# KAN window layer: identity sum of the K1 part as runs, the K2 part added by VectorE, SiLU in place on the columns-first copy, and another instruction order

## The reference

```
def _fastkan(x, ln_g, ln_b, ws, wb, bb):
    ln = _layernorm(x, ln_g, ln_b)
    basis = jnp.exp(-((ln[..., None] - GRID) / DENOM) ** 2)      # 8 bases
    return basis.reshape(*basis.shape[:-2], -1) @ ws.T + jax.nn.silu(x) @ wb.T + bb
...
y = _layernorm(wins, pn_g, pn_b)                                # windows of 8 x 8 pixels, PN
a = fastkan K1 of y, regrouped along the rows of a window
d = fastkan K2 of y, regrouped along the columns of a window
e = fastkan K3 of y
z = fastkan K4 of (a + d + e)
out = z + wins
```

## Time and profile before

| | us |
|---|---|
| median of 3 runs | 11005.96 |
| lowest and highest | 11001.5, 11026.69 |
| the profiled execution's own time | 10993.59 |
| its span, first to last instruction | 10991.8 |

### The profile page before, as it was taken

One profiled execution on the slowest core, in us unless ns is written; L12 is line 12 of the kernel. 1 busy time (PEld: TensorE's weight loads), 2 busy tenths in 40 slices (PEclk: granted clock), 3 DMA queues, 4 the chain that ended last, 5 costly groups with the idle time before them and its releaser, 6 DMA issues. The chain is left out here.

```text
span 10991.8 us, 350519 instructions
## 1 busy us (share of the span) xinstructions
PE 9088.7 (83%) x158376; PEld 4584.7 (42%) x158376; DVE 8630.6 (79%) x7794; ACT 7545.8 (69%) x5712; POOL 0.2 (0%) x4
## 2 busy tenths in 40 slices
PE   0898879996665798788888888888888888888788
PEld 0344333333443686344444444444444444444344
DVE  6777756666776587688888888888888888888788
ACT  0555545554552554688888888878888888887689
POOL 0000000000000000000000000000000000000000
PEclk9999989997887999799999999999999999999899
DMA  7999879995673586455555555555555555555566
GB/s 287 250 259 257 234 217 264 266 259 214 271 276 107 171 278 227 93 105 110 112 112 106 107 105 106 105 108 109 109 111 106 105 106 109 109 110 94 159 208 203
DMA packets 1196529, 1825.48 MB, mean 166 GB/s; under 512 B 135328, under 2 KB 956448, under 8 KB 1124768
## 3 DMA queue, kind: packets, MB, share of 16 engines
q1 hardware_dynamic: 1195040, 1803.05, 64.6%
HBM read 717.78 MB, written 411.04 MB: 103 GB/s over the span
## 5 line engine op out<-in xcount | busy, mean ns | idle before, releaser
L2008 DVE SCALAR_TENSOR_TENSOR ex<-ratio,ex 128x2048 f32<-128x2048 f32 x1536 | 3504.4, 2290 | 226.7 <-ACT ratio L1910 134.7
L2129 PE MATMUL out<-ex,kan_basis 32*32 32x512 f32 x65536 | 2563.7, 624 | 321.8 <-DVE ex L2008 129.2
L2129 PEld LDWEIGHTS out<-ex,kan_basis 32*32 32x32 f32 x65536 | 1073.3, 105 | 1466.3 <-issue 801.5
L556 PE MATMUL conv<-uc,w 128*32 128x512 f32 x12288 | 1447.4, 597 | 17.1 <-DMA uc<-u 16.6
L1902 ACT ACTIVATE ex<-ex 128x2048 f32<-128x2048 f32 x512 | 975.6, 1905 | 2.9
L463 ACT ACTIVATE v<-conv,cb 128x512 f32<-128x512 f32 x512 | 350.8, 685 | 905.9 <-PE conv L556 414.5
L556 PEld LDWEIGHTS conv<-uc,w 128*32 128x32 f32 x12288 | 483.1, 109 | 735.4 <-issue 678.0
L2262 DVE TENSOR_TENSOR d<-xt 128x2313 f32<-128x2313 f32 (+2 forms) x256 | 621.7, 2494 | 83.3 <-PE acc L2316 82.9
L2316 PE MATMUL acc<-d,weights 32*32 32x512 f32 x16384 | 627.5, 600 | 70.9 <-issue 64.2
L1896 ACT ACTIVATE ex<-kin,offset 128x2048 f32<-128x2048 f32 x256 | 511.3, 1997 | 130.5 <-PE out L2129 115.0
L2080 PE MATMUL norm<-sq,c_kan_ones 128*32 128x128 f32 x10240 | 393.5, 297 | 212.1 <-DVE z L1984 151.3
(11 more groups left out here) (276 smaller groups left out, 14899.0 us busy)
## 6 DMA issues: line engine op xcount, KB each, us to landing
uc<-u SPq DMA_DIRECT2D x2048, 129.0 KB, 3.6
xt<-in_x SPq DMA_DIRECT2D x128, 1024.0 KB, 7.4
t<-v SPq DMA_DIRECT2D x128, 1024.0 KB, 9.6
back_k<-ku SPq DMA_DIRECT2D x1024, 128.0 KB
xt<-in_x SPq DMA_DIRECT2D x32, 2048.0 KB, 7.4
xt<-t SPq DMA_DIRECT2D x64, 1024.0 KB, 7.1
tt<-t SPq DMA_DIRECT2D x64, 1024.0 KB, 11.9
x<-x SPq DMA_DIRECT2D x64, 1024.0 KB, 4.9
```

Of the source, the lines that this page charges most:

```text
L556: last = m.matmul(conv[QUAD * b:QUAD * b + QUAD, k % 2, :], w_sb[:, o, d, :], uc[:, h, b, 2 * p:2 * p + 2, d:d + COLS], start=(d == 0), st ...
L2008: v.scalar_tensor_tensor(base_buffer(kind, n, t), ratio[:], LARGEST, base_buffer(kind, n - 1, t), ALU.min, ALU.mult).then_inc(grown[kind], 1)
L2129: last = m.matmul(out[rows(i), g, :], k["kan_basis"][rows(g), kind - 1, n, :], base[rows(g), cols(i)], start=(n == 0), stop=(n == BASES - ...
```

## The change

1. K3's identity product takes B (the K1 part, contiguous) instead of D; DVE's evacuation of K3 adds D, read with the 1 KB step, instead of B. The waits go with them: K3's products wait for K1's part, the evacuation for K2's, and SP's conditions for overwriting B and D change places.
2. `turn_u` is gone. In its place ACT applies SiLU to `turned` in place (`silu_turned`), contiguous, when K2's y has been fed. It needs the SiLU table set.
3. K3's square moves from DVE to ACT.
4. All positions are new, and `STAGES` is 6 instead of 5.

```diff
-MOVE = {PN: 380, K1: 673, K2: 744, K3: 694, K4: 1138}
+MOVE = {PN: 640, K1: 962, K2: 1032, K3: 971, K4: 1431}
...
-EVACUATE = {K1: 922, K2: 1014, K3: 1040, K4: 1365}
+EVACUATE = {K1: 1214, K2: 1261, K3: 1171, K4: 1623}
...
-PRODUCT = {K1: (921, 922, 938, 948, 950, 953, 959, 963),
-           K2: (985, 986, 987, 989, 993, 1003, 1007, 1008),
-           K3: (1115, 1124, 1125, 1128, 1135, 1136, 1144, 1165),
-           K4: (1274, 1286, 1288, 1296, 1299, 1300, 1301, 1305)}
-SILU = {PN: 617, K4: 1132}
-TURN_Y, TURN_U, BETA, MEASURE = 626, 803, 518, 1331
-TURN_Y_BY_ACT = False
-TURN_U_BY_ACT = True
-LOAD_X, LOAD_R, STORE = 168, 1009, 1203
-FEED_Y, FEED_U, BACK = {K1: 451, K2: 495}, {K1: 531, K2: 734}, {K1: 768, K2: 769}
+PRODUCT = {K1: (996, 998, 1000, 1022, 1026, 1033, 1037, 1042),
+           K2: (1062, 1065, 1074, 1089, 1103, 1126, 1137, 1138),
+           K3: (1193, 1194, 1196, 1205, 1218, 1226, 1232, 1233),
+           K4: (1397, 1410, 1415, 1416, 1431, 1432, 1438, 1441)}
+SILU = {PN: 894, K4: 1424}
+TURN_Y, SILU_TURNED, BETA, MEASURE = 743, 1092, 620, 1545
+LOAD_X, LOAD_R, STORE = 176, 1111, 1270
+FEED_Y, FEED_U, BACK = {K1: 541, K2: 565}, {K1: 729, K2: 759}, {K1: 929, K2: 981}
-SQUARED_BY_ACT = (PN, K1, K2, K4)
+SQUARED_BY_ACT = (PN, K1, K2, K3, K4)
-STAGES = 5
+STAGES = 6
...
                 if kind == K1:
-                    wait_both(sp, evacuated[K3], t, evacuated[kind], t + 1)
+                    wait_both(sp, used, silu_used(K3, t - 1), evacuated[kind], t + 1)
                 else:
-                    wait_both(sp, used, silu_used(K3, t - 1), evacuated[kind], t + 1)
+                    wait_both(sp, evacuated[K3], t, evacuated[kind], t + 1)
...
-            def turn_u(t):
-                act.wait_ge(u_ready[PN], t + 1)
-                act.wait_ge(kin_loaded[K2], 128 * t + 128)
-                a.activation(columns_first(turned[:]), rows_first(U[:, t % 2]), ACT.Identity).then_inc(copied_u, 1)
...
+            def silu_turned(t):
+                act.wait_ge(copied_y, t + 1)
+                act.wait_ge(kin_loaded[K2], 128 * t + 128)
+                tables(SILU_SET)
+                a.activation(turned[:], turned[:], ACT.Silu).then_inc(copied_u, 1)
...
-                    dve.wait_ge(back_loaded[K1], 128 * t + 128)
-                    v.scalar_tensor_tensor(Z[:], out_flat, out_b(kind, t % 2), B[:], ALU.add, ALU.add).then_inc(evacuated[kind], 1)
+                    dve.wait_ge(back_loaded[K2], 128 * t + 128)
+                    v.scalar_tensor_tensor(by_rows(Z[:]), by_rows(out_flat), out_b(kind, t % 2), D[:].rearrange("p (x rw) -> p rw x", x=BAND),
+                                           ALU.add, ALU.add).then_inc(evacuated[kind], 1)
...
-                    pe.wait_ge(back_loaded[K2], 128 * t + 128)
-                    by_rows = D[:].rearrange("p (x rw) -> p rw x", x=BAND)
+                    pe.wait_ge(back_loaded[K1], 128 * t + 128)
                     for i in range(CHUNKS):
-                        m.matmul(out[:, i, :], c["ident"][:], by_rows[:, BANK // BAND * i:BANK // BAND * i + BANK // BAND, :],
-                                 start=False, stop=False)
+                        m.matmul(out[:, i, :], c["ident"][:], B[:, cols(i)], start=False, stop=False)
```

More of the change, by code:

```diff
@@ L1609 @@
 UNITS = 256
-CENTER = {PN: 437, K1: 727, K2: 749, K3: 732, K4: 1179}
-MOVE = {PN: 380, K1: 673, K2: 744, K3: 694, K4: 1138}
[L1612 to L1617, removed]
-EVACUATE = {K1: 922, K2: 1014, K3: 1040, K4: 1365}
@@ L1630 @@
-SILU = {PN: 617, K4: 1132}
-TURN_Y, TURN_U, BETA, MEASURE = 626, 803, 518, 1331
-TURN_Y_BY_ACT = False
-TURN_U_BY_ACT = True
-LOAD_X, LOAD_R, STORE = 168, 1009, 1203
-FEED_Y, FEED_U, BACK = {K1: 451, K2: 495}, {K1: 531, K2: 734}, {K1: 768, K2: 769}
+CENTER = {PN: 454, K1: 798, K2: 902, K3: 837, K4: 1267}
+MOVE = {PN: 640, K1: 962, K2: 1032, K3: 971, K4: 1431}
+SQUARE = {PN: 655, K1: 967, K2: 1045, K3: 1001, K4: 1433}
+VARIANCE = {PN: 487, K1: 867, K2: 950, K3: 884, K4: 1294}
+LOG = {PN: 658, K1: 991, K2: 1127, K3: 1020, K4: 1444}
@@ new lines @@
+ROOT = {PN: 841, K1: 1002, K2: 1144, K3: 1088, K4: 1468}
+SPREAD = {PN: 677, K1: 908, K2: 995, K3: 922, K4: 1319}
+SCALE = {PN: 577, K1: 806, K2: 924, K3: 813, K4: 1270}
+EVACUATE = {K1: 1214, K2: 1261, K3: 1171, K4: 1623}
+RATIO = {K1: 1145, K2: 1186, K3: 1341, K4: 1489}
+ANCHOR = {K1: (1121, 1159), K2: (1173, 1219), K3: (1294, 1370), K4: (1482, 1522)}
+EXP = {K1: (1139, 1171), K2: (1176, 1220), K3: (1300, 1376), K4: (1484, 1538)}
+GROW = {K1: {1: 877, 2: 905, 3: 931, 5: 934, 6: 939, 7: 983},
+        K2: {1: 1000, 2: 1003, 3: 1010, 5: 1019, 6: 1030, 7: 1032},
+        K3: {1: 1064, 2: 1071, 3: 1088, 5: 1093, 6: 1104, 7: 1107},
+        K4: {1: 1292, 2: 1294, 3: 1296, 5: 1297, 6: 1303, 7: 1313}}
@@ L1751, in rows_first, with by_rows @@
             return tile_.rearrange("p (rw x) -> p x rw", x=BAND)
+        def by_rows(tile_):
+            return tile_.rearrange("p (rw x) -> p rw x", x=BAND)
         class Round:
@@ L1805, in give_back @@
                 if kind == K1:
+                    wait_both(sp, used, silu_used(K3, t - 1), evacuated[kind], t + 1)
+                else:
                     wait_both(sp, evacuated[K3], t, evacuated[kind], t + 1)
-                else:
-                    wait_both(sp, used, silu_used(K3, t - 1), evacuated[kind], t + 1)
                 for i in range(G):
@@ L1870, in silu @@
                         act.wait_ge(ku_loaded[K1], 128 * (t - 1))
-                        act.wait_ge(copied_u, t - 1)
                     act.wait_ge(normed, t + 1)
@@ L1921, in round_ @@
                             silu(kind, t)
-                    for position, by_act, step in ((TURN_Y, TURN_Y_BY_ACT, turn_y), (TURN_U, TURN_U_BY_ACT, turn_u)):
-                        if by_act and (t := now.due(u, position)) is not None:
-                            step(t)
+                    if (t := now.due(u, SILU_TURNED)) is not None:
+                        silu_turned(t)
                     for kind in NORMS:
@@ L1953, in turn_y @@
                 v.tensor_copy(columns_first(turned[:]), rows_first(Y[:, t % 2])).then_inc(copied_y, 1)
[L1955 to L1958, removed]
             def move(kind, t):
@@ L2035, in round_ @@
                                 grow(kind, n, t)
-                    for position, by_act, step in ((TURN_Y, TURN_Y_BY_ACT, turn_y), (TURN_U, TURN_U_BY_ACT, turn_u), (BETA, False, add_beta), (MEASURE, False, measure)):
-                        if not by_act and (t := now.due(u, position)) is not None:
+                    for position, step in ((TURN_Y, turn_y), (BETA, add_beta), (MEASURE, measure)):
+                        if (t := now.due(u, position)) is not None:
                             step(t)
```

## The result

The changed kernel took 10971.39 us (median of 8 runs, 10945.95 to 10992.42) against 11019.81 us before (8 runs). The ratio is 0.9953, 95% interval 0.9940 to 0.9967: some 52 us less. Forecast were 10730 us and a range of 10620 to 10940. The sign was right, the size was not, and the time lies outside the range.

What follows compares the result with a forecast made beforehand. No engine saturated: the 89.4 us round is a loop of waits across three engines. 63 x -4.8 = -302, plus 25 for the fill = -277 us: 10993.6 to 10717, or 10730 on the median's scale; range 10620 to 10940.

Steps and rivals of the forecast that it cites:

- Where the round closes: At K3's evacuation DVE and ACT wait and PE alone is the path; the identity as runs saves PE 3.45 us.
- The prices: Per-operation costs: identity 3.70 us, K3's evacuation 3.95, SiLU in place 1.91, two more table loads a round at 1.28 each.
- Rival B: In K3's evacuation the step in DVE's read is hidden: 1.6 us less per round, 10630 us; chance 0.20.
- rival E: Between K4 and K3 both new table switches stall ACT another 1.28 us each: 10892 us; chance 0.03.
- cover of 2.7 us: At K3's evacuation K2's result lands at 79.6, DVE needs it at 82.3; this narrower margin was costed at nothing.
- the walk: One round stepped through the engine queues between ends of K3's last product: 82.3 us new against 87.1 old, 4.8 less.
- Rival D: K2's part, behind load_x, lands 7 us late for K3's evacuation: slower, 11170 us; chance 0.08.
- The walk, at log PN: On ACT the walk priced two new table loads, +2.57 us per round, and nothing for the load at log PN.
- The square: K3's square moved to ACT: DVE loses 2.29 us and its 3.88 us wait, ACT gains 1.9 us.
- Fill, +25 us: First tile until K4's evacuation: stretched by 0.46 rounds more, at 50 us a round in the fill, +25 us.
- the 2 us by which the walk missed the old round: The walk ended the old round at 87.1 against the trace's 89.3; the lack was placed where PE's granted clock falls.

Runs made afterwards that it cites:

- part 1 alone: The kernel before with only part 1 of the change, every position as before: 10866.28 us, ratio 0.9867.
- both repairs: The changed kernel with K2's result given back ahead of load_x and log's table load ahead of its waits: 10741.89 us, ratio 0.9760 to before.
- Repairing it gave 115 us: The changed kernel with SP giving K2's result back ahead of load_x instead of behind it: 10838.14 us, ratio 0.9848 to before.
- Repairing it gave 83 us: The changed kernel with log's exp table load issued ahead of log's waits instead of behind them: 10863.24 us, ratio 0.9877 to before.
- two comparisons: Kernel before plus parts 1 to 3, old order: 0.9903; both repairs with K3's square back on DVE: 0.9781, against 0.9760 for both repairs.

## Where the prediction held and where it failed

*Where the round closes.* Right. PE's run from the identity to K3's last product was the path: part 1 alone gave 2.11 us per round, where the forecast prices give 3.45 - 1.6 = 1.85, and 2.05 with the evacuation as measured.

*The prices.* Right. Identity 3.70 us (3.70 forecast), evacuation 3.74 (3.95 forecast, between the bounds 2.35 and 4.47), loads 261 of 1.28 us, SiLU 1.91. No drain shows behind a load: log PN starts 0.01 us after it. Rival B (the step is hidden) and rival E (a switch stalls for more than its load) fall. The Trainium skill's rule that access across 16-byte lines pays (SBUF — State Buffer, "Door 1: The DMA port swizzle") agrees with 3.74 against 2.35.

*The DMAs, "cover of 2.7 us", costed at nothing.* This step failed. The forecast took 5.2 us from the last issue to landing, the median of load_x, and it was the wrong row. K2's result landed 8.9 us after its last issue, 3.7 us more. The issue was late as well: it ended 6.6 us before K3's last product did, where the walk had 7.9. Together 2.7 - 1.3 - 3.7 = -2.3 us: the cover was gone, and DVE waited 134.6 / 63 = 2.1 us per round. What is different about load_x is not settled. It is another transfer (four issues of 256 KB, against eight of 128 KB), and in the kernel before it stood in SP's queue alone, with only a store behind it:

```profile
7055.84 1.73 SPq L1777 DMA_DIRECT2D x<-x  x4
7057.62 0.43 SPq L1787 DMA_DIRECT2D x<-x_to_x  x1
```

K2's result has a megabyte ahead of it and one behind it. But with both repairs, away from load_x, the DMAs that give back still have a median of 9.0 us. No run tells the kind of transfer from its neighbours. Rival D had named the mechanism and given it 0.08, but only for the case that it made the kernel slower. Its smaller form, which eats part of the gain, was the one that came, and it had no chance of its own. Repairing it gave 115 us.

*The walk, at log PN.* This step failed too. The prediction prices the two new loads, but has no term for the load that was there already, whose place changed. In the old order it stood ahead of the exp of K1, with log PN some 14 us later. In the new order log PN comes first, and in the code `tables(EXP_SET)` stands behind log's waits, so that the load starts when the variance is done. I had let it run while ACT waited for the variance, which the recorded milestones do not spell out. The row for it was there: the load before SiLU of y starts only after its 5.34 us wait. Repairing it gave 83 us.

The two together are 212 us. Milestones, counted from the end of K3's last product (7048.60 + 3.58 = 7052.2 in the changed kernel, 7049.53 + 3.51 = 7053.0 with both repairs): the first product of K1 starts at 4.1 in the walk, 6.1 measured, 3.9 with both repairs; K1's last product ends at 20.1 in the walk, 25.4 measured (7077.6) and 19.7 with both repairs (7072.7). With both repairs the walk holds there to half a microsecond.

*The square.* The 2.29 us of DVE and its 3.88 us wait were counted as gain beyond the identity's. That failed as well: they were slack, and two comparisons, one in the old order and one in the new, show no effect beyond noise.

*Fill, +25 us.* Did not come, and its divisor of 4.5 rounds stands on no row. K4's first evacuation starts at 4624.6 us against 4625.2:

```profile
L1911 ACT ACTIVATE x_to_x<-out,end_b x64: 1947/1967/1969, 4624.6 to 10192.2; 128x2048 f32<-128x2048 f32 x64
```

Positions say nothing of latency here; only waits do.

*What is left.* With both repairs the round is 85.7 us against 84.6. I had put the 2 us by which the walk missed the old round down to the clock alone. Part of it is something else, the stops described at the end. In the round shown above with both repairs, K2's last product ends at 38.6 us (39.2 in the walk) and K4's last at 63.1 (60.3). Between them PE stops twice with nothing to wait for, 2.66 us in all:

```profile
7100.77 2.12 PE L2118 MATMUL out<-ex,kan_basis 32*32 32x512 f32 x38 [1.87 <-issue]
7110.52 2.20 PE L2118 MATMUL out<-ex,kan_basis 32*32 32x512 f32 x47 [0.79 <-issue]
```

How much of the round the stops cost as a whole was not measured by a run.

The parts together: part 1 -146 us, part 2 +32, part 3 +7 (no more than noise), the new order +55, make the -52 measured. In the new order 212 us lay in two places, and neither was visible in busy times.

## What to carry to other kernels

Take the landing time of a DMA from a row of the same kind of transfer with the same neighbours in the queue; where no row has it, give a cover as small as the 2.7 us here a good chance of failing. When a table load (or any set-up) is issued lazily, put it ahead of the semaphore wait; behind it, it adds its full length to the chain that it follows. And a new order should be tried against the old one with the same operations: here part 1 alone in the old order (0.9867) beat the whole change (0.9953).

## What was not expected of the hardware

PE stands still in the middle of groups of 32 equal matmuls, where the profile shows nothing that it waits for. In the changed kernel:

```profile
7105.03 0.71 PE L2081 MATMUL norm<-roots,c_sel 32*128 32x128 f32 x12
7108.03 1.04 PE L2081 MATMUL norm<-roots,c_sel 32*128 32x128 f32 x20 [2.29 <-issue]
```

The stretches between consecutive such stops, as windows (x: matmuls, then weight loads):

```profile
7108.03:7194.39 86.36, 74.38 (x1527) 33.58 (x1527) 72.97 (x36) 71.93 (x49) 0.00 (x0) 0.94 0.54 107
7194.39:7231.95 37.56, 32.82 (x637) 15.85 (x637) 31.02 (x15) 32.10 (x22) 0.00 (x0) 1.00 0.59 102
7231.95:7287.81 55.86, 47.51 (x1019) 20.53 (x1018) 48.29 (x25) 47.10 (x32) 0.00 (x0) 0.91 0.55 114
```

They hold 3054, 1274 and 2037 matmuls and weight loads: 12, 5 and 8 times about 255. So these stops go by count of instructions, not by time. In the 1770 us from 6000 on (20 rounds) PE's timeline has 21 idle times of 0.5 to 5 us labelled "issue", 44.5 us in all, before the change, and 32, 78.6 us, after it; with both repairs 27, 61.7 us. So 2 to 4 us of each round are such stops, and a walk by durations and semaphores has none. The changed kernel has 1.7 us a round more of them than the kernel before; how much of that is in its 55 us for the new order no run tells. The Trainium skill (Runtime: NRT & Kernel Launch, "Instruction fetch mechanics") says that an engine's instructions are refilled in blocks of 256 and that crossing a block is mostly hidden. The distances agree with the 256. If these stops are such crossings, "mostly hidden" does not hold for this stream of short matmuls. That code loading is the cause is argued from the distances; no run tested it.

With a strided second input the VectorE operation takes 3.74 us instead of 2.35 for 2048 elements, less than the doubling that PE (7.16 against 3.70) and ACT (4.03 against 1.91) show.
